# Group work of a mixture-of-experts kernel split into quarters behind its tiles, and beta added four graphs at a time

## The reference

```python
x = x + gnn(layernorm(x), adj, ...)             # first stage
# second stage: u = layernorm(x)
gate_logits = u @ gate_w + gate_b
topk_vals, topk_idx = top_k(gate_logits, 2); topk_w = softmax(topk_vals)
h = relu(einsum('bsh,ehf->bsef', u, w1) + b1)   # 16 experts, F = 256
expert_out = einsum('bsef,efh->bseh', h, w2) + b2
y = u + sum(topk_w * selected expert_out)
x = x + layernorm(y) * gamma + beta
```

## Time and profile before

| | before |
|---|---|
| median of 3 runs | 888.42 us (888.24 to 890.37) |
| profiled execution, its own time | 883.51 us |
| its span, first to last instruction | 881.0 us |
| PE busy | 771.3 us (88%), 4739 matmuls |
| DVE, ACT, POOL busy | 70%, 60%, 63% |
| tile stage | some 423 to 841 us |
| tail behind the last scatter | 846 to 881 us |

### The profile page before, as it was taken

How to read it: one execution, slowest core, us unless ns; L and a number is a source line. 1 busy time by engine, 2 the same in 40 slices (tenths; PEclk the granted TensorE clock), 3 DMA queues, 4 the chain that set the end, 5 groups by cost and what they waited for, 6 DMA issues and landing times. The chain is left out here.

```text
span 881.0 us, 20052 instructions
## 1 busy us (share of the span) xinstructions
PE 771.3 (88%) x4739; PEld 590.4 (67%) x4740; DVE 619.3 (70%) x2448; ACT 527.7 (60%) x1123; POOL 550.9 (63%) x572
## 2 busy tenths in 40 slices
PE   5999999999999999961899999988878888888844
PEld 4577777777777777751677777766656666666621
DVE  3688999999999998866455554567665666665648
ACT  2599999999999999871233333444443343343435
POOL 2005777777677777675777777777765565565630
PEclk9999999999999999995899999999998889898969
DMA  5323343333333332215777667888887778767636
GB/s 153 97 73 109 120 122 121 118 121 116 105 118 116 119 95 75 74 58 146 215 207 199 199 206 238 260 239 231 247 239 215 225 215 236 216 198 221 188 131 215
DMA packets 104175, 145.23 MB, mean 165 GB/s; under 512 B 17537, under 2 KB 56855, under 8 KB 104119
## 3 DMA queue, kind: packets, MB, share of 16 engines
q1 hardware_dynamic: 84582, 109.16, 44.0%
q0 software_dynamic: 17344, 34.13, 11.1%
q10 hardware_dynamic: 2192, 1.31, 0.5%
HBM read 99.67 MB, written 46.81 MB: 166 GB/s over the span
## 5 line engine op out<-in xcount | busy, mean ns | idle before, releaser
L471 POOL DMA_INDIRECT combined<-tout,tdest x286 | 285.7, 999 | 129.9 <-issue 74.0
L458 POOL DMA_INDIRECT dispatched<-rows,slot_i x256 | 259.5, 1014 | 165.5 <-issue 145.6
L795 ACT ACTIVATE hid<-bank,wts 128x256 f32<-128x256 f32 x286 | 119.6, 469 | 236.5 <-PE bank L651 235.8
L1119 DVE SCALAR_TENSOR_TENSOR tout<-bank,gate,tin 128x128 f32<-128x128 f32 x286 | 86.9, 345 | 157.9 <-PE bank L666 156.7
L666 PE MATMUL bank<-wts,hid 128*128 128x128 f32 x1144 | 175.5, 299 | 0.0
L666 PEld LDWEIGHTS bank<-wts,hid 128*128 128x128 f32 x1144 | 147.2, 201 | 17.8 <-issue 1.5
L651 PE MATMUL bank<-tut,wts 128*128 128x256 f32 x572 | 155.4, 396 | 0.0
L506 PEld LDWEIGHTS bank<-w_sb,work 128*128 128x128 f32 x1024 | 123.1, 194 | 17.9 <-issue 14.6
L506 PE MATMUL bank<-w_sb,work 128*128 128x128 f32 x1024 | 126.3, 277 | 2.1 <-ACT work L774 2.1
L500 PE MATMUL bank<-agg,w_sb 128*128 128x512 f32 x256 | 124.8, 610 | 0.0
L651 PEld LDWEIGHTS bank<-tut,wts 128*128 128x128 f32 x572 | 103.0, 201 | 8.7
(11 more groups left out here) (159 smaller groups left out, 1046.8 us busy)
## 6 DMA issues: line engine op xcount, KB each, us to landing
wts<-in_w_exp SPq DMA_DIRECT2D x143, 257.0 KB
tin<-dispatched SPq DMA_DIRECT2D x143, 132.0 KB
moe<-combined SPq DMA_DIRECT2D x32, 512.0 KB, 4.6
xs<-in_x SPq DMA_DIRECT2D x32, 256.0 KB, 3.2
adj_sb<-in_adj_t SPq DMA_DIRECT2D x32, 256.0 KB, 3.3
rms_b<-r_row SPq DMA_DIRECT2D x32, 256.0 KB, 3.2
out<-agg SPq DMA_DIRECT2D x32, 256.0 KB, 4.2
combined<-tout,tdest POOLq DMA_INDIRECT x286
```

The costliest lines, as they stand in the source:

```text
L458: nc.gpsimd.indirect_dma_start(dispatched, bass.IndirectOffsetOnAxis(slot_i[:, k, n:n + 1], 0), rows[:, k, n // TOPK, n % TOPK, :], None). ...
L471: nc.gpsimd.indirect_dma_start(combined, bass.IndirectOffsetOnAxis(tdest[:, k, a:a + 1], 0), tout[:, k, a, :], None, bounds_check=TOK * TO ...
L795: last = nc.scalar.activation(hid[:, n % 2, c, :], hid_ps[n % 2][:, c * TILE:(c + 1) * TILE], ACT.Relu, bias=wts[:, k, F + FC * D + c:F + ...
L1119: last = nc.vector.scalar_tensor_tensor(out=tout[:, k, a, :], in0=exp_ps[n % 2][:, a * D:(a + 1) * D], scalar=gate[:, n % 2, a:a + 1], in1 ...
```

## The change

`mixed` calls `post_step` behind every tile and names the quarter. The first argument of each part of a post_step is now also a test for its quarter:

- DVE: quarter 0 has the reciprocal, the offset and the sum of the two rows; quarter 1 the statistics; quarter 2 gamma; quarter 3 the add of `xs`.
- ACT: quarter 1 normalises graphs 0 and 1 of a group, quarter 2 graphs 2 and 3 (and raises `p_n`) and makes the root of the next group.
- SP: load and store both in quarter 3, where they were.
- PE: `tut_ps` has two banks (0 and 1), transposes of tile n wait for the copy of tile n-2. `y_ps` is moved from the banks 1, 6, 7 to 0, 1, 2.
- DVE: beta is added to four graphs at a time, in tile_steps 7 to 38 and only in those without group work (`m == 1`); the mixed steps have no such add.
- The loop of tiles alone has 5 turns instead of 6; steps 37 to 42 are unrolled.

```diff
-        tut_ps, hid_ps, exp_ps = bank[0], bank[2:4], bank[4:6]
-        y_ps = (bank[1], bank[6], bank[7])
+        tut_ps, hid_ps, exp_ps = bank[0:2], bank[2:4], bank[4:6]
+        y_ps = bank[0:RING]
...
             def mixed(i, t, g):
                 for k in range(RING * GB):
                     tile_step(i, t + k, 2)
-                    if k % GB == GB - 1:
-                        post_step(i, g + k // GB)
-
-            pipeline(eng, tile_step, first, 7, (MIX_FROM - 7) // RING2, MIX_FROM, RING2)
+                    post_step(i, g + k // GB, (k % GB,))
+
+            pipeline(eng, tile_step, first, 7, NG // RING2, MIX_FROM, RING2)
...
-            def post_step(i, t):
+            def post_step(i, t, quarters=range(GB)):
                 g = t + 2
-                if has(i, g):
+                if 3 in quarters and has(i, g):
...
-                    if n >= 1:
-                        pe.wait_ge(t_ut, count(i, n, 1, RING2 * m))
+                    if n >= 2:
+                        pe.wait_ge(t_ut, count(i, n - 1, 1, RING2 * m))
...
+                for half in range(2):
+                    if 1 + half in quarters and has(i, g):
+                        k = g % RING
+                        if half == 0:
+                            if g >= RING:
+                                act.wait_ge(p_g, count(i, g - RING + 1))
+                            act.wait_ge(p_nb, count(i, g + 1))
+                            act.nop(nofuse=True)
+                        for j in (2 * half, 2 * half + 1):
+                            last = nc.scalar.activation(n3[:, k, j, :], y_of(i, g, k)[:, j, :], ACT.Identity,
+                                                        bias=nb[:, 0, k, j:j + 1], scale=rs[:, 0, k, j:j + 1])
+                        if half == 1:
+                            last.then_inc(p_n, 1)
...
-                if has(i, b, NB):
-                    row = xs[:, bass.ds(count(i, b, 1, RING2 * m), 1), :].rearrange("p o d -> p (o d)")
-                    nc.vector.tensor_tensor(row, row, beta_sb[:], ALU.add).then_inc(beta_in, 1)
+                if m == 1 and has(i, b, NG):
+                    xb = xs[:, bass.ds(count(i, b, GB, RING2), GB), :]
+                    nc.vector.tensor_tensor(xb, xb, beta_sb[:, :].unsqueeze(1).broadcast_to([P, GB, D]), ALU.add)\
+                        .then_inc(beta_in, 1)
...
-                    dve.wait_ge(beta_in, count(i, g + 1, GB))
+                    dve.wait_ge(beta_in, count(i, g + 1))
```

More of the change, by code:

```diff
@@ L636, in tile_step @@
                     pe.wait_ge(tin_in[k], count(i, n // RING2 + 1, 16, m))
-                    if n >= 1:
-                        pe.wait_ge(t_ut, count(i, n, 1, RING2 * m))
+                    if n >= 2:
+                        pe.wait_ge(t_ut, count(i, n - 1, 1, RING2 * m))
                     for a in range(TH):
-                        last = nc.tensor.transpose(tut_ps[:, a * P:(a + 1) * P], tin[:, k, a, 0:D],
+                        last = nc.tensor.transpose(tut_ps[n % 2][:, a * P:(a + 1) * P], tin[:, k, a, 0:D],
                                                    ident[:])
@@ L798, in tile_step, with post_step @@
                     last.then_inc(t_relu, 1)
-            def post_step(i, t):
+            def post_step(i, t, quarters=range(GB)):
                 g = t - 1
[L802 to L811, removed]
+                for half in range(2):
[11 more added lines that the diff above has]
+                            last.then_inc(p_n, 1)
                 g = t
-                if has(i, g):
+                if 2 in quarters and has(i, g):
                     k = g % RING
@@ L816, in post_step @@
                     nc.scalar.activation(sd[:, 0, k, :], bn[:, 0, k, :, 2], ACT.Sqrt, bias=ln_eps[:, 0:1],
-                                         scale=1.0 / D)\
-                        .then_inc(p_sd, 1)
+                                         scale=1.0 / D).then_inc(p_sd, 1)
             tiles_and_groups(act, tile_step, post_step, -1)
@@ L1100, in tile_step @@
                         dve.wait_ge(t_h, count(i, n - 1, 1, RING2 * m))
-                    nc.vector.tensor_copy(tut[:, n % 2, :], tut_ps[:, 0:TILE]).then_inc(t_ut, 1)
+                    nc.vector.tensor_copy(tut[:, n % 2, :], tut_ps[n % 2][:, 0:TILE]).then_inc(t_ut, 1)
                 n = t - 1
@@ L1122, in tile_step, with post_step @@
                     last.then_inc(t_out, 1)
-            def post_step(i, t):
+            def post_step(i, t, quarters=range(GB)):
                 g = t - 1
-                if has(i, g):
+                if 0 in quarters and has(i, g):
                     k = g % RING
@@ L1129, in post_step @@
                     nc.vector.reciprocal(rs[:, 0, k], sd[:, 0, k, :]).then_inc(p_rs, 1)
-                g = t - 1
-                if has(i, g):
-                    k = g % RING
                     dve.wait_ge(p_rs, count(i, g + 1))
@@ L1137, in post_step @@
                 g = t
-                if has(i, g):
+                if 0 in quarters and (i is not None or 0 <= g < MIXED):
+                    k = g % RING
+                    dve.wait_ge(moe_in[k], count(i, g // RING + 1, 16, 1))
+                    nc.vector.tensor_tensor(moe[:, k, :, 0, :], moe[:, k, :, 0, :], moe[:, k, :, 1, :],
+                                            ALU.add).then_inc(p_sum, 1)
+                if 1 in quarters and has(i, g):
                     k = g % RING
                     if summed_by_dve(i, g):
-                        dve.wait_ge(moe_in[k], count(i, g // RING + 1, 16, 1))
-                        nc.vector.tensor_tensor(moe[:, k, :, 0, :], moe[:, k, :, 0, :], moe[:, k, :, 1, :],
-                                                ALU.add).then_inc(p_sum, 1)
                         dve.wait_ge(p_sum, count(i, g + 1))
@@ L1157, in post_step @@
                         .then_inc(p_g, 1)
-                g = t - 2
-                if has(i, g):
+                if 3 in quarters and has(i, g):
                     k = g % RING
```

## The result

The changed kernel takes 849.81 us (median of 4 runs, 847.91 to 851.63) against 889.19 us for the kernel before in the same comparison (4 runs, 888.24 to 890.37). The ratio is 0.9556, with a 95% interval of 0.9528 to 0.9585: 39.4 us less. The profiled execution is the run of 851.63 us, its span 849.5.

A forecast was written before the change was run, and what follows sets the result against it. PE waiting behind DVE's group block and SP waiting for `p_n` bound the mixed stretch; afterwards SP would. 883.5 less 36.5 gives 847.0 us profiled, plus 4.9 to the median: 852 us, forecast range 848 to 857.

The forecast's parts named there:

- the slow tile: Mixed loop: after PE's gap a tile takes 4.0 us at granted clock 0.76, 1.6 us more per group; expected to go.
- The price of the bank: PE transposes: a second bank alone hides 0.38 us of a late copy, one pair of transposes, and not more.
- What is late next: Mixed stretch: SP becomes the bound at 10.9 us per group, against GpSimd 10.3 and PE 9.5.
- The 33.0 us of SP's wait: SP's queue, before each group's `moe` load: waits for ACT's `p_n`, 33.0 us in 20 cases, should go.
- The sum: Whole kernel: last tile load at 793.2, its transposes at 796.4, unchanged tail; gain 36.5 us, 847.0 profiled, 852 us median.
- The 1.2 us that I gave back for POOL: Last scatter: 1.2 us taken off the 37.7 us gain, since GpSimd will be closer to its own bound.
- A: Tile stage: SP is quicker than it looks, GpSimd's scatters set the end; gain 43 to 44 us, 845 us; chance 0.11.
- B: Mixed stretch: DMA engines or the clock take part of the gain back; 862, or 856 to 868 us; chance 0.18.
- C: DVE's quarter 0: the sum waits for the `moe` load, PE behind it; 876 us, 870 to 885; chance 0.07.
- D: Mixed stretch: TensorE stays at 1.2 GHz for long, making the kernel slower; about 905 us; chance 0.06.
- E: SP's queue: the fourth tile's completion holds SP, not `p_n`; its wait only moves to L367; 888 us; chance 0.05.

The follow-up runs named there:

- the delayed kernels: Changed kernel and kernel before, each with a second table read by SP for each of 135 tiles: 926.28 us (ratio 1.046) and 926.87 us (1.047).

## Why the prediction was right, and where its sum was off

**The cause.** DVE's 3.15 us in one piece, the copy queued behind, PE waiting 2 us, the slow tile after it: right. The quarters alone give 34.7 us, and PE's wait for `tut` falls to 0.2 us. The slow tiles went too, if not all: between 537 and 840 us the eight second products of a tile, 1.16 us at the full clock, took 1.6 us or more 12 times before and 4 times after. The price of the bank (0.38 us per group) was right where it can be seen. That the moved beta is hidden in the tiles alone was right: that stretch has the same pace as before. That it is needed for the quarters to fit was wrong at SP's pace.

**What is late next.** The 33.0 us of SP's wait went, as the step had it, and SP then sets the pace: the delayed kernels show it, 75 of 76 us. But SP is not the only bound. The sum treated POOL as slack behind it, with 10.3 against 10.9 us per group. The average hid that SP is a little quicker than POOL in the unrolled groups (10.1 us per group) and slower in the loop (11.5). In the unrolled code DVE waits for old scatters, 4.4 us in the longest case, with PE idle for 3.9 us behind it, and half the scatters give 11 us.

**The sum**, between profiled executions: 36.5 us predicted, 883.51 - 851.63 = 31.9 measured. Term by term: the last tile load was to start at 793.2 and started at 796.8, 3.6 us later. The load of tile 46 starts at 530.4, where it started at 534.0: 1.0 us of that because the first load of all came earlier, and 2.5 for the unrolled loads, where I had 1.7. From there to the last load it is 266.4 us (11.1 per group) against the 260.9 that I had, 5.5 more. SP's wait for a free buffer is 3.6 of them, 6.4 us where there were 2.8, which I had carried over unchanged; the other 1.9 are left for SP's own steps, which no run splits further. Together -1.0 - 0.8 + 5.5 = 3.7, the 3.6 us from above with its rounding. From the last load to its transposes I had 3.2 us and it took 6.0 (796.8 to 802.8). A load shortly before took 4.9 us to land, in the timeline of the end of the stage:

```profile
788.98 0.39 SPq L366 DMA_DIRECT2D tin<-dispatched  x1
...
793.89 0.44 PE L639 MATMUL bank<-ident,tin 128*128 128x128 f32 x2 [1.89 <-DMA tin<-dispatched]
...
795.44 2.08 PE L665 MATMUL bank<-wts,hid 128*128 128x128 f32 x8
```

PE stood for 1.89 us, and its next second products were slow (2.08 us). So PE was behind there: 2.8 us. The 1.2 us that I gave back for POOL were not needed (5.5 us between last STT and last scatter, before and after). 3.6 + 2.8 - 1.2 = 5.2 us, which is the 5.1 by which the last scatter (814.5) came later than the predicted 809.4. The tail (35.0 against 35.1 us) is unchanged. All this is one trace of each kernel: in the second trace of the changed kernel tile load 46 to the last takes 264.0 us.

**The median** came out at 849.8 against 852, closer than the sum deserves, and that is luck. I carried over 4.9 us as the distance of a profiled execution from the median. The profiled execution of the kernel before (883.51 us) is none of the four of this comparison; it lies 5.7 us below their median, but 1 to 2 us below the medians of the three other comparisons. That of the kernel after lies 1.8 us above its median. That distance is spread and no constant: the gain by medians was 39.4 us in this comparison and 34.6 in the second.

**The rivals.** A (POOL's floor) is part of the truth: the time is 5 us above its 845. B came only in traces: the clock rose to 0.97, PE's 2.38 us held at a DMA share of 0.86, and four tiles had slow second products. (Its upper end was added wrongly: 12 x (13 - 10.9) is 25 us lost and not 15, so 877 us instead of 868.) C did not come: DVE waits for no `moe` load. D did not come: the granted clock is higher than before, and even in the changed kernel with the delayed SP, where PE waits for `tin` ahead of 71 of the 143 tiles, it was 0.89 from 627 to 760 us, (1 - 0.89)/0.5 = 22% of the time at the low level, where D needed 42% of the tiles. (D's own sum gives 907 us at the least, not 905.) E did not come: the waits that went did not come back at L366, except for 3.6 us.

## What to carry to other kernels

Work that is done once per several steps should be cut into parts that fit into the spare time of each step; here that was worth 35 us, and what the second buffer and the moved adds around it were still worth once it was done (nothing to 8 us) these runs do not settle. When an engine stops being the bound, look for the next one among the queues that only issue: add up what SP's instructions take between its waits, and compare that with the step of the others; waits of an issuing queue are slack that vanishes with the change. Where two bounds are as close as here (SP 10.1 to 11.5 us per group, POOL 10.3), expect that easing one shows only up to the other. An issue moved to a computing engine has to be looked at in every stage in which that engine runs it.

## What the runs showed of the hardware that was not expected

- SP needs 2.3 to 2.6 us to issue two loads with addresses from a table (the read of the table alone takes 0.48 us), and 3.73 us with two more transfers in the loop. PE's whole step takes 2.38. The Trainium skill, "DMA: Bandwidth & Descriptors", section "Issuing engines are not separate DMA queues", calls the time to initiate a DMA usually small relative to the DMA itself. For the issuing instruction alone this trace agrees (0.38 us for `tin`, against 2.38 from its start to the transposes that waited for it); with the read of the table and the work on addresses around it, it is the bound in this kernel, and 76 us more of it made the kernel 75 us slower.
- Once the engines are relieved, the DMA engines are busy 0.84 to 0.86 of the time, at 248 to 257 GB/s, and PE's steps are still 2.38 us.
- The granted clock of TensorE in the mixed stretch went from 0.91 to 0.97, but these runs do not show that the end of the 2 us gap did that. From 627 to 790 us it was 0.91 before, 0.90 with beta alone, 0.93 with the bank alone and 0.98 in the changed kernel. With both bank and beta and no quarters it was 0.97 as well, though PE still waited for the copy in 12 cases of up to 1.7 us there:

```profile
627.00:790.00 163.00, 137.53 (x798) 103.94 (x797) 97.91 (x358) 67.21 (x171) 105.37 (x107) 0.97 0.83 236
```
